# FFN0's end on one Trainium2 core: first blocks ahead, projections behind the down products, q's low weights in four pieces, shifts on ScalarE

## What is computed

```
x = x + _L0_xattn_ref(_layernorm(x, axis=-1), ctx_4096, ...)
x = x + _L0_ffn_ref(_layernorm(x, axis=-1), ..., L0_ffn_ln_gamma, L0_ffn_ln_beta)
x = x + _L1_xattn_ref(_layernorm(x, axis=-1), ctx_4096, ...)
x = x + _L1_ffn_ref(_layernorm(x, axis=-1), ...)
```

```
h = jax.nn.relu(jnp.einsum('bsh,hi->bsi', hidden_states, up_w)) ** 2
shared_out = jnp.einsum('bsi,ih->bsh', h, down_w)
...
return _layernorm(shared_out + routed_out, ln_gamma, ln_beta)
...
q = (query @ Wq + bq).reshape(B, L, NKV, G, HDIM)
k_, v_ = jnp.split(kv @ Wkv + bkv, 2, axis=-1)
```

## Time and profile before

| | |
|---|---|
| median of three runs | 1169.54 us (1169.13 to 1169.9) |
| the profiled execution | 1169.32 us, of which the span from first to last instruction is 1167.5 |
| PE busy | 1127.2 us, 97% of the span |
| DVE busy | 560.2 us, 48% |
| ACT busy | 513.9 us, 44% |
| POOL busy | 371.1 us, 32% |

### The profile page before, as it was taken

One profiled execution on the slowest core, in us unless ns is written; L12 is line 12 of the kernel. 1 busy time (PEld: TensorE's weight loads), 2 busy tenths in 40 slices (PEclk: granted clock), 3 DMA queues, 4 the chain that ended last, 5 costly groups with the idle time before them and its releaser, 6 DMA issues.

```text
span 1167.5 us, 15309 instructions
## 1 busy us (share of the span) xinstructions
PE 1127.2 (97%) x5478; PEld 905.2 (78%) x5478; DVE 560.2 (48%) x1021; ACT 513.9 (44%) x1390; POOL 371.1 (32%) x250
## 2 busy tenths in 40 slices
PE   6999999999999999987999999999999999999997
PEld 4787787787787688865888888888888888888774
DVE  5374364364368443388433524335243352433665
ACT  5474374374277332333623516235162351623631
POOL 3151052053043353555412404124041240412440
PEclk9999999999999999998999999999999999999998
DMA  8011011010000221110111101101011110110001
GB/s 251 14 41 28 1 40 27 0 45 9 0 19 1 91 90 36 55 37 1 55 36 36 54 0 54 36 36 54 0 54 36 36 54 0 39 36 1 13 4 72
DMA packets 22646, 43.55 MB, mean 37 GB/s; under 512 B 14069, under 2 KB 14325, under 8 KB 19925
## 3 DMA queue, kind: packets, MB, share of 16 engines
q1 hardware_dynamic: 22612, 43.12, 11.3%
HBM read 41.02 MB, written 2.10 MB: 37 GB/s over the span
## 4 chain that ended last, share of the span: by engine, by line
PE 87%; DVE 6%; ACT 2%; POOL 2%; issue 2%; DMA 0%; SPq 0%; DVEq 0%
PE work L482 14%; PE work L484 14%; PE work L483 14%; PE work L544 8%; PE yb L482 5%; PE yb L484 5%; PE yb L483 5%; PE pt L554 4%; PE ov L484 3%; PE ov L482 3%; PE ov L483 3%; PE pt L484 3%; PE pt L483 3%; PE pt L482 3%; DVE minus_mean L1408 1%
## 5 line engine op out<-in xcount | busy, mean ns | idle before, releaser
L1150 POOL TENSOR_TENSOR prob<-prob,exp_rcp 128x512 f32<-128x512 f32 (+1 forms) x96 | 127.3, 1326 | 586.7 <-DVE exp_rcp L1331 586.7
L968 ACT ACTIVATE prob<-work,neg_max 128x128 f32<-128x128 f32 (+1 forms) x384 | 149.2, 407 | 69.1 <-DVE neg_max L1355 68.4
L482 PE MATMUL work<-xT_hi,q_hi 128*128 128x512 f32 x416 | 169.1, 407 | 5.1 <-DVE xT_lo L1420 5.1
L484 PE MATMUL work<-xT_hi,q_lo 128*128 128x512 f32 x416 | 165.1, 397 | 0.0
L483 PE MATMUL work<-xT_lo,q_hi 128*128 128x512 f32 x416 | 164.8, 396 | 0.0
L544 PE MATMUL work<-kT,qT 128*128 128x128 f32 (+1 forms) x768 | 128.2, 310 | 1.0 <-DVE qT L1265 0.9
L544 PEld LDWEIGHTS work<-kT,qT 128*128 128x128 f32 (+1 forms) x768 | 114.1, 191 | 14.2 <-issue 1.6
L921 ACT ACTIVATE pT_hi<-pt 128x512 fp32r<-128x512 f32 x128 | 73.8, 603 | 84.0 <-PE pt L554 83.5
L1388 DVE TENSOR_TENSOR oT_lo<-ov,oT_hi 32x128 fp32r<-32x128 f32 (+2 forms) x160 | 67.4, 421 | 78.3 <-ACT oT_hi L927 76.9
L1355 DVE TENSOR_REDUCE neg_max<-work 128x4 f32<-128x512 f32 (+1 forms) x96 | 83.0, 865 | 40.1 <-PE work L544 38.2
L482 PE MATMUL yb<-o_hi,oT_hi 128*128 128x512 f32 x224 | 94.0, 419 | 4.8 <-DVE oT_lo L1388 4.7
(11 more groups left out here) (189 smaller groups left out, 2113.2 us busy)
## 6 DMA issues: line engine op xcount, KB each, us to landing
q_raw<-in_l_q SPq DMA_DIRECT2D x8, 1024.0 KB, 4.8
o_raw<-in_l_o SPq DMA_DIRECT2D x8, 1024.0 KB, 4.8
kv_raw<-in_l_kv SPq DMA_DIRECT2D x8, 515.0 KB, 3.3
o_raw<-in_l_o SPq DMA_DIRECT2D x4, 768.0 KB, 4.3
q_raw<-in_l_q SPq DMA_DIRECT2D x16, 144.0 KB, 2.5
qT<-in_ctxT SPq DMA_DIRECT2D x4, 512.0 KB, 6.8
x<-in_x SPq DMA_DIRECT2D x2, 1024.0 KB, 11.4
q_raw<-in_up SPq DMA_DIRECT2D x2, 1024.0 KB, 6.2
```

Of the source, the lines that this page charges most:

```text
L482: pe.matmul(dst, l_hi, r_hi, start=first and k == 0, stop=False)
L484: mm = pe.matmul(dst, l_lo, r_hi, start=False, stop=last and k == n - 1)
L968: e = act.activation(prob[:, i % 2, g * L.keys:(g + 1) * L.keys], s[:, g, :], ACT.Exp, bias=neg_max[:, i % 2, g:g + 1], accum_out=exp_sum[ ...
L1150: pool.tensor_tensor(p, p, exp_rcp[:, b % 2, :].unsqueeze(2).broadcast_to([P, G, L.keys]), ALU.mult)\
```

## The change

Four edits, which belong together at FFN0's end, and one of which reaches further:

1. Blocks 0 to 3 of the two norms get their own order on DVE, ACT and POOL, and the normalised blocks of N[2] have four buffers (relu and h_f) instead of two.
2. On PE the eight down products stand together. Behind them come the transposes of blocks 0 and 1, a k/v projection, the transposes of 2 and 3, the other three k/v projections, then the q projections with the transposes of 4 and 5 behind the first, and those of 6 and 7 behind the last. The wait for the last xT_lo moves into the attention loop, behind the first scores.
3. POOL makes q's low weights in four pieces of 512 columns between the rstd of blocks 2 to 4, and all eight additions of bo behind the last rstd.
4. `shift` is gone from DVE for all norms but N[0]: in `normalise_x` ACT copies minus the mean, then scales it by rstd, each a 128 x 1 instruction. This holds for N[1] and N[3] too.

The diff, cut to its core:

```diff
+            def transpose_pair(n, b):
+
+                for c in (b, b + 1):
+                    transpose_x(n, c, (n.lo, c - 1) if c >= 2 else (f0.route, 1))
...
-            mlp_half(1, N[2])
+            mlp_half(1)
+            transpose_pair(N[2], 0)
+            project(L1, S1, 0, "kv", 0, (f0.relu, 16))
+            transpose_pair(N[2], 2)
+            for u in range(1, 4):
+                project(L1, S1, 0, "kv", u, (f0.relu, 16))
             pe.wait_ge(N[2].lo, 4)
-            for u in range(2):
-                project(L1, S1, 0, "q", u, evac_of(L1, S1, "kv", u))
-                transpose_x(N[2], 4 + u, (N[2].lo, 3 + u))
+            project(L1, S1, 0, "q", 0, evac_of(L1, S1, "kv", 0))
+            transpose_pair(N[2], 4)
+            project(L1, S1, 0, "q", 1, evac_of(L1, S1, "kv", 1))
             project(L1, S1, 0, "q", 2, evac_of(L1, S1, "kv", 2))
-            transpose_x(N[2], 6, (N[2].lo, 5))
-            transpose_x(N[2], 7, (N[2].lo, 6))
             project(L1, S1, 0, "q", 3, evac_of(L1, S1, "kv", 3))
-            drained(N[2])
+            transpose_pair(N[2], 6)
             attention(L1, S1, N[3])
...
             def normalise_x(n, b, src, dst=None):
 
-                act.wait_ge(n.shift, b + 1)
+                if n is N[0]:
+                    act.wait_ge(n.shift, b + 1)
+                else:
+                    own = minus_mean[:, b:b + 1]
+                    act.wait_ge(n.var, b + 1)
+                    act.activation(own, mean_var[:, b, 0:1], ACT.Copy, scale=-1.0).then_inc(n.minus, 1)
+                    act.wait_ge(n.rstd, b + 1)
+                    act.wait_ge(n.minus, b + 1)
+                    act.activation(own, own, ACT.Copy, scale=rstd[:, b:b + 1]).then_inc(n.shift, 1)
+                    act.wait_ge(n.shift, b + 1)
...
-            split_lo(q_lo, q_raw, q_hi, 2048, P, q_hi_done, q_lo_done, L1.q0)
+            def lower_q(k):
+
+                pool.wait_ge(q_hi_done, L1.q0 + 1)
+                at = slice(k * HID, (k + 1) * HID)
+                return pool.tensor_tensor(q_lo[:, at], q_raw[:, at], q_hi[:, at].bitcast(F32), ALU.subtract)
...
-                if norm is not None and i >= 4:
-                    shift(norm, i - 4)
```

More of the change, by code:

```diff
@@ L364, in xn_buf @@
         def xn_buf(n, b):
[L367 to L368 removed]
+            if n is N[2]:
+                return (relu, h_f)[b // 2 % 2][:, b % 2, :]
             if n is N[0]:
@@ L595, in attention_head @@
                         scores(L, S, it, i)
+                        if L.double and i == 0:
+                            pe.wait_ge(N[2].lo, NB)
                         for u in L.q_steps[i]:
@@ L787, in _, with mlp_half @@
                          for k in range(2)]).then_inc(f0.down, 1)
-            def mlp_half(hf, norm=None):
+            def mlp_half(hf):
                 pe.wait_ge(q_lo_done, hf + (UP + 1))
@@ L1231, in _, with scale_acc @@
             mlp_half(1)
-            split_lo(q_lo, q_raw, q_hi, 2048, P, q_hi_done, q_lo_done, L1.q0)
-            pool.wait_ge(bo_loaded, 16)
[L1234 to L1248, removed]
+            def scale_acc(b):
+                pool.wait_ge(NA.xn, b + 1)
+                pool.tensor_tensor(acc[:, b, :], acc[:, b, :], gamma[:, :], ALU.mult).then_inc(f0.scaled, 1)
+            def lower_q(k):
+                pool.wait_ge(q_hi_done, L1.q0 + 1)
+                at = slice(k * HID, (k + 1) * HID)
+                return pool.tensor_tensor(q_lo[:, at], q_raw[:, at], q_hi[:, at].bitcast(F32), ALU.subtract)
+            rstd_of(NA, 0)
+            scale_acc(0)
+            rstd_of(NA, 1)
+            scale_acc(1)
+            rstd_of(NA, 2)
+            rstd_of(N[2], 0)
+            scale_acc(2)
+            rstd_of(NA, 3)
+            rstd_of(N[2], 1)
+            scale_acc(3)
+            rstd_of(N[2], 2)
+            lower_q(0)
+            rstd_of(N[2], 3)
+            lower_q(1)
+            rstd_of(NA, 4)
+            lower_q(2)
+            scale_acc(4)
+            lower_q(3).then_inc(q_lo_done, 1)
+            for b in range(5, NB):
+                rstd_of(NA, b)
+                scale_acc(b)
+                rstd_of(N[2], b - 1)
+            rstd_of(N[2], NB - 1)
+            pool.wait_ge(bo_loaded, 16)
+            for b in range(NB):
+                pool.wait_ge(N[2].xn, b + 1)
+                pool.tensor_tensor(x[:, b, :], x[:, b, :], bo_bc[:, :], ALU.add).then_inc(bo_added, 1)
             attention(L1, S1, N[3], KT * ZH, 2048, 1024, 2048)
@@ L1346, in head @@
                         lin_lo(i - NB - 1)
-                if norm is not None:
-                    shift(norm, NB - 1)
             def negative_max(L, S, it, b, last):
@@ L1500, in statistics_x, with add_and_measure, measure @@
                 statistics(N[2], x, b)
[L1503 to L1516, removed]
+            def add_and_measure(b):
+                add_down(1, b)
+                measure(b)
+            def measure(b):
+                dve.wait_ge(f0.added, 2 * NB + b + 1)
+                statistics(NA, acc, b)
+            add_and_measure(0)
+            add_and_measure(1)
+            add_and_measure(2)
+            add_norm(0)
+            statistics_x(0)
+            add_down(1, 3)
+            measure(3)
+            add_norm(1)
+            statistics_x(1)
+            for b in (2, 3):
+                add_down(1, b + 2)
+                add_norm(b)
+                statistics_x(b)
+            add_down(1, 6)
+            measure(4)
+            add_down(1, 7)
+            norm_lo(N[2], 0)
+            norm_lo(N[2], 1)
+            measure(5)
+            add_norm(4)
+            norm_lo(N[2], 2)
+            norm_lo(N[2], 3)
+            statistics_x(4)
             evacuate(L1, S1, 0, ("kv", 1))
+            measure(6)
+            add_norm(5)
+            statistics_x(5)
+            measure(7)
             add_norm(6)
```

43 lines of the change are left out of this document (24 added, 19 removed).

## The result

The changed kernel takes 1155.08 us (median of 4 runs, 1154.51 to 1155.72) against 1169.72 beside it: 0.9877 of the time (95% interval 0.9864 to 0.9891), 14.6 us less. The forecast was 16.7 less. Its profiled execution took 1155.23 us, its span 1153.4 against 1167.5.

The account below looks back on a forecast made before the run. PE at FFN0's end, held by a wait chain of DVE's minus_mean, POOL's rstd and DVE's statistics. Stretch -16.0, FFN1 -1.2, FFN0 +0.5: -16.7 us from 1169.54 to 1152.8; range 1150 to 1155.5 (0.72), wider 1150 to 1159.

Parts of the forecast that it names:

- The ledger of waits, half clock and products: PE, first down product to head 0's scores: 63.2 of 65.1 us accounted for, including products 44.8, transposes 2.8, waits 12.7.
- The walk of the first blocks: Blocks 0 to 3 of x at FFN0's end: ready at about 501.8, 505.4, 507.7 and 510.0 us.
- the 5.1 us wait: PE's wait for the first half's last xT_lo; three k/v products (8.4 us) were to hide it, so it goes.
- The sum of the stretch: First down product to head 0's scores: 47.6 + 0.3 + 0.3 + 0.2 + 0.7 = 49.1 against 65.1, so -16.0 us.
- The moved wait: PE's wait for the last xT_lo, moved behind head 0's first scores: about 0.7 us lost there.
- the failed step: Ahead of FFN0: two of eight pairs stand directly ahead of an output split PE waits for, 0.5 us more.
- N[3] was set at -1.2: Ahead of FFN1: about 1.9 us of PE's waits go, ACT's 0.47 comes back once or twice.
- Pair of tiny copies: ACT's two [128,1] copies for each block's shift: 0.19 + 0.28 = 0.47 us, at most 1.03.
- Pieces of q_lo at nothing: POOL's split of q's low weights in four pieces of about 1.2 us: hidden, ending about 514, wanted at 522.
- The first: Rival: the chain stays part of the bound at FFN0's end, 2.5 to 7 us lost, 1155 to 1160; chance 0.15.
- The second: Rival: 16 pairs ahead of FFN0 and FFN1, all on PE's path, cost 7.5 us, giving 1161; chance 0.05.
- The third: Rival: scaled copies make ACT change function tables at each normalisation; at 3.5 us a pair, about 1179; slower: chance 0.03.

Follow-up runs that it names:

- b_n3: The changed kernel, but ahead of FFN1 DVE makes the shifts again, as before; 1155.57 us.
- d_order: The changed kernel, but DVE makes the 16 shifts between FFN0's last eight down products and head 0's scores; 1163.91 us, 0.9953 of before.
- e_shifts: The kernel before, old order and one-piece q split, but ACT makes the 16 shifts of N[2] and NA; 1153.71 us, 0.9865 of before.
- k_tile: e_shifts plus an otherwise unused tile of 128 bytes per partition, zeroed once, allocated behind minus_mean; 1152.92 us.

## Why the prediction was right, and where it wasn't

**What bounds the stretch: right.** The ledger of waits, half clock and products held, and so did the diagnosis that DVE's own shifts hold the chain. The earlier trace rows begin at 440, where PE's products are all of the chain; that PE leads no line of it holds from 487 to 552 us, in the kernel before:

```profile
by line: DVE minus_mean L1408 21.4%; POOL rstd L1190 16.5%; DVE stats L1399 14.6%; issue 14.1%; DVE mean_var L1401 4.5%; DVE xT_lo L1420 3.7%; DVE var_eps L1403 3.6%; ACT q_hi L883 2.9%; DVE x L1496 2.7%; DVE vT L1265 2.3%; DVE acc L1484 2.
```

The shifts on ACT alone take the 66.01 to 51.20. How much of this is DVE's standing and how much the shifts' own 16.5 us, no run separates.

**The walk of the first blocks: right.** Blocks 0 to 3 of x were set at 501.8, 505.4, 507.7 and 510.0; ACT ends them at 503.39, 506.96, 509.31 and 511.67. Of these 1.6 to 1.7 us 1.44 are the later start of the down products, 488.64 for 487.20. Of the loads set for DVE, POOL and ACT, 35, 23 and 26 us, POOL's was too low: the three stretches above add up to 37.1, 36.9 and 30.2. It cost nothing that shows, since all stay below PE's 50.4.

**How the gain was shared out: wrong.** The forecast let the 5.1 us wait go by the order on PE (three k/v products that hide xT_lo) and the early start of blocks 0 and 1 by the pieces of q_lo. With ACT's shifts and none of that, 4.4 of the 5.1 go, and block 0 of x ends 17.2 us behind the first down product, where it was 20.1 (14.8 in the changed kernel): early enough for its transpose. The gains don't add up: 7.2 by the order, 14.8 by the shifts, 15.0 by both, since each alone moves the same chain out of PE's way and PE's own work is a floor for all. No rival in the forecast asked what one part alone would do.

**The sum of the stretch: 1.0 us short.** Up to the second q step the forecast comes to 49.1 + 0.88 (the scores) = 50.0; measured 51.02. Terms, from the starts in PE's timeline: eight transposes take 0.40 each, not 0.35, because in the earlier trace rows the 0.35 came from one block that was followed by a product at once, and in a pair the first block takes 0.44 (+0.4); the seventh down product waits and restarts for 0.56, not 0.3 (+0.26); the first product behind transposes takes 0.07 more, three times (+0.2); blocks 5 and the scores together +0.2. The moved wait is the one term that was fair: 1.51 from the scores to the q step, where 0.88 + 0.7 was set.

**The other two norms: the larger miss.** N[1] was set at +0.5 (two pairs ahead of an output split) and cost 1.7: the failed step counted two pairs of eight on PE's path, and four of them inside the head cost 1.27 alone. N[3] was set at -1.2 and gave 0.05 the wrong way: the waits of 1.0 and 0.9 in the earlier trace rows do hang on DVE's shifts, for they went with them and are back in b_n3. What was set too low is what comes in their place: waits of 2.0 for pT_lo and 1.2 for a normalised block, where ACT's pairs were priced at one or two times 0.47. That ACT's longer queue makes these is argued from their releasers, not shown by a run. Together these two are 2.4 us, the stretch 1.0; against them stand 0.8 us that the profile after was better in places that vary from run to run. That part is luck: without it the profiled execution would have taken 1156.0 us, above the 1155.5 at which the forecast's narrower range ends.

**Pair of tiny copies: right.** Estimated 0.19 + 0.28, measured 0.197 + 0.295. The Trainium skill, "ScalarE: Activation LUTs", section "What ACT_TABLE_LOAD costs", gives 186 ns, plus 0.83 for each column, for an instruction with immediate operands and 93 ns more for each per-partition one, by estimate 187 and 280 here; the two rows lie some 5% above. The rule weighed in the forecast, that tiny operations are dearest on ScalarE, is true of the instruction (0.49 for a pair against 0.16 on an undisturbed DVE) and didn't decide: the 16 shifts took 16.5 us on DVE in place, and in d_order with a quieter DVE still 0.52 each. The Trainium skill, "SBUF — State Buffer", section "SBUF: two separate sides", has a DVE instruction with two SBUF inputs and a GpSimd instruction that reads SBUF exclude each other; the 1.24 us shift behind POOL's 1.29 us product fits that, and no run here took the port alone away.

**Pieces of q_lo at nothing, the moved wait: right for this order.** Undone, they cost 1.6 and 1.2. They repair what the new order needs; the old one has no need of the pieces. The late additions of bo and the four buffers of N[2] were not tried by themselves.

**Rivals.** The first (part of the chain still binds, 1155 to 1160) has the measured time at its edge but not its mechanism: PE waits 0.2 us for a block. Its price for pairs of 1.03 us, 2.5 lost at the least, was 1.1 in this order with pairs of 1.07. The second (pairs bite elsewhere) is what happened, at one place of two and at 1.7 in place of 7.5. The third (ACT changes its function tables): before and after alike the trace has one load of function tables, in its first 2 us, and none between ACT's later instructions.

## What to carry to other kernels

When one engine stands in its own queue for a tiny step of a chain over several engines, move that step first, alone, and measure before anything is reordered: here that was worth 14.8 of 15.0 us, and the reordering only tightened covers. Change only the place that is bound: the same move in two other layer norms cost 1.7 us at one and nothing at the other. And parts of a change that remove the same chain must not be priced one by one and added up.

## What the runs showed of the hardware that was not expected

A tile of 128 bytes per partition that nothing reads, allocated behind minus_mean and ahead of the attention's tiles (qT, kT, vT, prob, pT, v, oT), makes L1's eight heads 0.8 us faster (589.02 us in e_shifts, 588.18 in k_tile), with the same order on every engine. It shows in all four kernels with the tile and in none of the ten without, and is spread over the whole head, some 0.1 us in each. It doesn't lie in waits: PE's idle time there is 2.87 us in e_shifts and 2.89 in k_tile. It lies in the steps from one matmul's start to the next, here summed over the eight heads for three kinds of step: 64 steps behind `ov<-pT_lo,v_hi` take 14.56 us in place of 14.81, 128 behind `yb<-o_lo,oT_hi` 29.74 in place of 29.94, while 128 behind `pt<-o_lo,pT_hi` take 29.81 in place of 29.69. That the tiles behind it start at other addresses is the likely way; which tile matters, and whether another size would do more, wasn't tried.
